# Cross attention and quantised feed-forward: seven block products in the last two token groups only, six groups as plain units

## The reference

```python
x = x + xattn(layernorm(x), ctx, Wq, Wkv)          # x: 2 x 2048 x 512, ctx: 2 x 128 x 512
h = act_qdq(layernorm(x))                          # 16-bit grid, one scale for the whole tensor
up   = act_qdq(h @ lpbq_dequant(w_up).T)           # weights 1536 x 512, 4 bits in blocks of 32
gate = act_qdq(h @ lpbq_dequant(w_gate).T)
gate = act_qdq(gate * fixed_qdq_u16(sigmoid(gate)))
o    = act_qdq(gate * up)
out  = x + o @ lpbq_dequant(w_down).T
```

## Time and profile before

| | us |
|---|---|
| median of 3 runs | 909.1 (908.61 to 911.49) |
| profiled execution | 906.48 |
| its span | 904.7 |
| TensorE, ScalarE, VectorE, GpSimd busy | 858.6, 593.1, 722.3, 202.6 |
| plain units | 130.3 to 258.6 |
| quads | 258.6 to 377.4 |
| up stage | 382.0 to 636.8 |
| first down pass and product | 645.0 to 731.5 |
| rest of the down projection | to the end |

### The profile page before, as it was taken

How to read it: one execution, slowest core, us unless ns; L and a number is a source line. 1 busy time by engine, 2 the same in 40 slices (tenths; PEclk the granted TensorE clock), 3 DMA queues, 4 the chain that set the end, 5 groups by cost and what they waited for, 6 DMA issues and landing times.

```text
span 904.7 us, 11995 instructions
## 1 busy us (share of the span) xinstructions
PE 858.6 (95%) x4072; PEld 423.6 (47%) x4072; DVE 722.3 (80%) x1009; ACT 593.1 (66%) x740; POOL 202.6 (22%) x170
## 2 busy tenths in 40 slices
PE   7999879999987999799999989999799989999998
PEld 5877554444433444344444434444344434444443
DVE  4879885689774868688996859857899997999892
ACT  2478776785673456689996859853689975455330
POOL 0099949499400088000000000000000000000000
PEclk9999979999999999999999999999999999999999
DMA  9822319753899558999439993799897897989872
GB/s 345 328 94 95 139 48 318 219 173 121 237 293 300 211 192 210 277 375 347 163 138 323 361 354 141 261 399 389 288 400 278 276 321 278 391 304 385 301 288 102
DMA packets 126469, 236.61 MB, mean 262 GB/s; under 512 B 48336, under 2 KB 66768, under 8 KB 124368
## 3 DMA queue, kind: packets, MB, share of 16 engines
q1 hardware_dynamic: 125264, 231.77, 73.5%
q10 hardware_dynamic: 1152, 4.19, 1.2%
HBM read 130.55 MB, written 95.42 MB: 250 GB/s over the span
## 4 chain that ended last, share of the span: by engine, by line
PE 59%; issue 14%; POOL 8%; DMA 6%; DVE 6%; ACT 3%; SPq 3%; POOLq 0%; ACTq 0%; DVEq 0%
PE ps L1091 27%; PE ps L1141 14%; PE ps L1042 8%; PE ps L1026 6%; PE ps L1168 3%; POOL big L858 2%; DMA big<-in_L_ffn_w_gate_dram 2%; DMA big<-big 2%; ACT big L1186 1%; POOL big L815 1%; POOL big L809 1%; DVE big L1756 1%; PE ps L1158 1%; POOL small L855 1%; DVE big L1730 1%
## 5 line engine op out<-in xcount | busy, mean ns | idle before, releaser
L1091 PE MATMUL ps<-big 128*128 (+1 forms) x1152 | 252.4, 383 | 7.1 <-DMA big<-big 4.6
L1091 PEld LDWEIGHTS ps<-big 128*128 128x128 f16 x1152 | 113.4, 99 | 146.0 <-issue 7.5
L1186 ACT ACTIVATE big<-ps 128x1024 f32<-128x1024 f32 (+2 forms) x142 | 113.9, 813 | 94.9 <-PE ps L896 25.5
L1026 PE MATMUL ps<-big 128*128 (+1 forms) x576 | 124.8, 379 | 4.1 <-ACT big L1186 3.7
L1141 PE MATMUL ps<-big 128*128 128x512 f16 x576 | 126.5, 382 | 2.3 <-DVE big L1961 2.3
L1042 PE MATMUL ps<-big 128*128 128x512 f16 x504 | 111.1, 383 | 7.7 <-DVE big L1801 5.7
L800 POOL PARTITION_ALL_REDUCE small<-small x8 | 3.3, 414 | 456.2 <-DVE small L1902 187.5
L1141 PEld LDWEIGHTS ps<-big 128*128 128x128 f16 x576 | 56.7, 99 | 71.7 <-issue 4.9
L1026 PEld LDWEIGHTS ps<-big 128*128 128x128 f16 x576 | 56.0, 98 | 72.7 <-ACT big L1186 4.6
L1122 PE MATMUL ps<-big 128*128 128x512 f16 x384 | 85.0, 384 | 5.1 <-ACT big L1471 5.1
L1042 PEld LDWEIGHTS ps<-big 128*128 128x128 f16 x504 | 49.4, 99 | 69.2 <-DVE big L1801 7.3
(11 more groups left out here) (117 smaller groups left out, 1310.5 us busy)
## 6 DMA issues: line engine op xcount, KB each, us to landing
big<-up_park SPq DMA_DIRECT2D x90, 512.0 KB, 6.5
big<-gate_park SPq DMA_DIRECT2D x48, 512.0 KB, 6.3
up_park<-big SPq DMA_DIRECT2D x48, 512.0 KB, 4.6
gate_park<-big SPq DMA_DIRECT2D x24, 512.0 KB, 2.9
gate_park<-big SPq DMA_DIRECT2D x48, 256.0 KB, 2.4
big<-in_x_dram SPq DMA_DIRECT2D x8, 1024.0 KB, 18.3
x_park<-big SPq DMA_DIRECT2D x8, 1024.0 KB, 3.9
product_park<-big SPq DMA_DIRECT2D x16, 512.0 KB, 5.6
```

The lines of the kernel that those rows point to most:

```text
L1026: mm = nc.tensor.matmul(unit_banks(n)[:, j], WG[:, x, a, k % 2, o:o + P], XT[:, g, b, k], start=(k == 0 and a + b == 0), stop=(k == KC - 1 ...
L1091: mm = nc.tensor.matmul(ps[:, b + j], WU[:, a, k, o:o + P], XT[:, g, c, k], start=(k == 0 and a + c == 0), stop=(k == KC - 1 and c == 1))
L1186: return nc.scalar.activation(dst, src, ACT.Copy)
```

## The change

Six groups are plain units and only groups 6 and 7 are quads: 36 units and 6 quads. The token sums of that one pair are made at units 24 to 26. Down pieces go to units 14, 17, 20, 23. Up weights are loaded behind units 27 to 30, their block maxima are taken at units 29 and 30, their scales at 31 and 33, and they are split at quads 1 to 4 and transposed at quads 2 to 5. A piece is now three blocks of 128 weight rows with all 512 columns (`up_rows`, `WU` and the loads are laid out for it); each piece has its own semaphore, and TensorE waits for piece 0, 1, 2, 3 at up units 0, 1, 3, 4, while ScalarE, VectorE and SyncE wait for all four (`up_turned`). At the quads' end gates 1 to 5 are fetched one by one, each behind the stores of its quad, with the last stores between them.

```diff
-FLAT_G = 4
+FLAT_G = 6
 FLAT = FLAT_G * UPG
-PAIRS = (NG - FLAT_G) // 2
-QUADS = PAIRS * UPG
+QUADS = UPG
 G_COLS = FLAT + 4 * QUADS
 SUM_AT = (8, 10, 13, 16)
 SPLIT_AT = (3, 5, 7, 9, 11, 16, 18)
-DOWN_AT = (14, 16, 19, 21)
-PARK_AT = (17, 19, 22, 24)
-TURN_AT = (19, 12)
-UP_AT = (7, 8, 9, 10)
+DOWN_AT = (14, 17, 20, 23)
+PARK_AT = (16, 19, 22, 25)
+TURN_AT = 25
+UP_AT = (1, 2, 3, 4)
+LOAD_AT = 27
+BLOCKS_AT = (29, 30)
+SCALE_AT = (31, 33)
+
+UP_PIECES = OC // 3
+UP_NEEDS = (0, 1, 3, 4)
...
-        WU = part(U0, 6144).bitcast(F16).rearrange("p (l k o) -> p l k o", l=2, k=KC)
+        WU = part(U0, 6144).bitcast(F16).rearrange("p (l h k c o) -> p l h k c o", l=2, h=UP_PIECES, k=KC, c=3)
...
+        def up_rows(l, c):
+            return natural_at(1, c // 3)[:, l].rearrange("p (k c d) -> p c k d", k=KC, c=3)[:, c % 3]
+
...
-        wu_turned, wd_turned = sem("wu_turned"), sem("wd_turned")
+        wu_0, wd_turned = sem("wu_turned"), sem("wd_turned")
+        wu_turned, WU_TURNED = [wu_0, wg_ld[1], wn_ld[2], wd_turned], (0, 16, 16, 16 * 2 * KC)
...
+        def up_turned(eng):
+            for h in range(UP_PIECES):
+                eng.wait_ge(wu_turned[h], WU_TURNED[h] + 32)
+
...
             def load_up_weights(k):
-                sp.dma_start(WN.rearrange("p (k c d) -> p k c d", k=KC, c=OC)[:, k],
-                             wu_in[:, k * P:(k + 1) * P].rearrange("(c p) d -> p c d", p=P)).then_inc(up_ld[k], 16)
+                sp.dma_start(WN.rearrange("p (c d) -> p c d", c=OC)[:, 3 * k:3 * k + 3],
+                             wu_in.rearrange("(c p) d -> p c d", p=P)[:, 3 * k:3 * k + 3]).then_inc(up_ld[k], 16)
...
+                if LOAD_AT <= u < LOAD_AT + KC:
+                    load_up_weights(u - LOAD_AT)
...
-                if q == 0:
-                    park_down_weights(KC - 1)
-                if q < 2:
-                    load_up_weights(2 * q)
-                    load_up_weights(2 * q + 1)
-                if q >= QUADS - 4:
-                    if q == QUADS - 4:
-                        sp.wait_ge(q_mm, Q_MM + done_p7(UPG * (PAIRS - 1) - 1))
-                        sp.wait_ge(t_lo, T_LO + 4 * PAIRS)
-                    turn_up_weights(q - QUADS + 4)
+                if q - 1 in UP_AT:
+                    if q - 1 == UP_AT[0]:
+                        sp.wait_ge(t_lo, T_LO + 4)
+                    turn_up_weights(UP_AT.index(q - 1))
...
             sp.wait_ge(q_mm, Q_MM + 7 * QUADS)
-            for x in (1, 3):
-                sp.wait_ge(c_st[x], C_ST + 16 * UPG)
-            for i in range(1, 6):
+            def fetch_late_gate(i):
+                for x in (1, 3):
+                    sp.wait_ge(c_st[x], C_ST + 16 * i + 16)
                 fetch_gate(i)
+
+            fetch_late_gate(1)
+            fetch_late_gate(2)
             for x in (2, 3):
                 park_half(QUADS - 1, x)
+            fetch_late_gate(3)
+            fetch_late_gate(4)
+            for x in (2, 3):
+                park_half_sign(QUADS - 1, x)
+            fetch_late_gate(5)
             for s in range(3):
                 sp.wait_ge(g_st[s], 16 * FLAT // 3)
             fetch_gate(6)
             fetch_gate(7)
-            for x in (2, 3):
...
-                            sp.wait_ge(wu_turned, 16 * 2 * KC)
+                            up_turned(sp)
...
-            pe.wait_ge(wu_turned, 16 * 2 * KC)
...
+                if n in UP_NEEDS:
+                    h = UP_NEEDS.index(n)
+                    pe.wait_ge(wu_turned[h], WU_TURNED[h] + 32)
...
+                if m == 1:
+                    copy(up_rows(0, c), WN[:, c * D:(c + 1) * D].rearrange("p (k d) -> p k d", k=KC)).then_inc(wt_hi, 1)
                 else:
-                    act.wait_ge(t_lo, T_LO + 4)
-                copy(natural(m, 0, c), WN[:, c * D:(c + 1) * D]).then_inc(wt_hi, 1)
+                    copy(natural(m, 0, c), WN[:, c * D:(c + 1) * D]).then_inc(wt_hi, 1)
...
-            act.wait_ge(wu_turned, 16 * 2 * KC)
+            up_turned(act)
...
+                if u in BLOCKS_AT:
+                    up_block_max(2 * BLOCKS_AT.index(u))
+                    up_block_max(2 * BLOCKS_AT.index(u) + 1)
+                if u == SCALE_AT[0]:
+                    block_scales(1)
+                if u == SCALE_AT[1]:
+                    common_scale(1, 3)
...
-                if 2 <= q < 4:
-                    up_block_max(2 * q - 4)
-                    up_block_max(2 * q - 3)
-                if q == 3:
-                    block_scales(1)
-                if q == 5:
-                    common_scale(1, 3)
```

More of the change, by code:

```diff
@@ L1046, in first_of @@
             def first_of(q, base):
[L1047 to L1048 removed]
+                g = FLAT_G
+                six(base + 1, q, WG[:, 1], XT[:, g, :, 2:4], True)
             def quad(q):
[L1051 to L1052 removed]
+                base, g, n = 4 * ((q + 1) % 2), FLAT_G, q
                 need(pe, c_ev, C_EV + 4 * (q - 1) if q > 1 else 0)
@@ L1344, in _ @@
                 nc.scalar.activation(sign_out[:, u % 2], gate_out[u % 3], ACT.Sign).then_inc(sign_ev, 1)
-                for pr in range(PAIRS):
-                    for j in range(4):
-                        if u == TURN_AT[pr] + j // 2:
-                            turn_hi(pr, j)
+                for j in range(4):
+                    if u == TURN_AT + j // 2:
+                        turn_hi(j)
                 if u % 2 and u < 2 * NG - 3:
```

90 lines of the change are left out of this document (39 added, 51 removed).

## The result

| | before | changed |
|---|---|---|
| median of the runs | 908.86 us (907.23 to 911.49) | 899.07 us (897.58 to 900.64), 4 runs |
| ratio | | 0.9885, 95% interval [0.9866, 0.9903] |
| profiled execution, its span | 906.48, 904.7 us | 900.64, 898.8 us |

Forecast were 904.6 us; measured were 899.1, close to rival A's 898.3. Faster, as forecast, but by 9.8 us where 4.5 stood, though inside the stated range of 897.5 to 909.0. The two profiled executions in the table lie nearer to each other (5.9 us) than the medians do (9.8 us), so places in time are compared with the second pair beside the first.

What follows compares the result with a forecast made beforehand. TensorE was taken to bound the gate stage, a ScalarE, VectorE and DMA chain the up stage to 541 us. Terms 7.8 - 3.2 - 2.7 - 6.4 = -4.5 us gave 904.6 us, range 897.5 to 909.0.

Steps and rivals of the forecast that it cites:

- rival A: Up stage: ScalarE's chain follows TensorE, so the early start is kept whole, 6.3 us; 898.3 us; chance 12%.
- Part 7: Up stage: row pieces start TensorE 6.3 us ahead, all given back before unit 30; 0 us, bounds 0 and -8.2.
- Part 1: Gate stage: 36 more matmuls at 0.2158 us each, all on the path; +7.8 us.
- Parts 2 and 3: Both plain-stage breaks shrink or go, -3.2 us (bounds 0, -3.7); the breaks entering the quads go, -2.7 us.
- Part 4: Quad 2: its 4.9 us break and 1.5 us of slow clock go as loads move; -6.4 us.
- Part 5: Plain stage: up-weight loads behind units 27 to 30 cause no break, with 8 us of cover; 0 us.
- Part 6: Quads: GpSimd's up blocks run from 309.5 to 350.6 us, 10.7 us before they are wanted; 0 us.
- the first sign of the prediction: TensorE's profile after: no break of a microsecond or more between 130 and 372 us.
- The sum to the quads' end: Parts 1 to 4 together, 7.8 - 3.2 - 2.7 - 6.4: the quads end 4.5 us earlier.
- The break before unit 30: Up stage: TensorE, ahead of ScalarE, waits 2.4 + 6.3 = 8.7 us there, the clock falling to 0.5.
- Rivals B and C: B: breaks move instead of going, 911.0 us, 14%. C: GpSimd's late blocks stop TensorE in quad 4, 914.9 us, 6%.

Runs made afterwards that it cites:

- the second pair: Both kernels run once more, unchanged, with profiles: before 908.76 us, ratio 1.0001; changed 897.43 us, ratio 0.9864.
- the spread loads: Kernel before with the four up-weight loads behind quads 0 to 3, block maxima and scales moved: 907.9 us, ratio 0.9976.
- the repeat: Changed kernel run once more, unchanged, for a second profile: 897.43 us, ratio 0.9864.
- the repeat of before: Kernel before run once more, unchanged, for a second profile: 908.76 us, ratio 1.0001.
- the version with early gates: Changed kernel with gates 39 and 40 fetched at up step 24 instead of 25: 893.83 us, then 895.74; waiting for all pieces too, 900.08.
- two loads at a time: Changed kernel with the four up-weight loads issued two behind unit 27 and two behind unit 28: 896.48 us in one run.

## Why the prediction was wrong

It was wrong in one term of the sum, Part 7; the others held within about two microseconds.

- **Part 1**, +7.8 us: right; the regular runs have the same 0.2158 us a matmul.
- **Parts 2 and 3**, -3.2 and -2.7: all three breaks went (3.7 and 2.7 us). The reason was half right: in the plain stage fewer token sums, not the new places, did it; for the entry no run tells.
- **Part 4**, -6.4: right. The break of quad 2 and its slow clock are gone, and the spread loads show that four loads in two quads made at least 4.4 of the 6.4 us.
- **Part 5**, 0: right, and with more room than the 8 us; a load took 4.6 us to land, 7.8 before.
- **Part 6**, 0: GpSimd's times to a microsecond. But I costed the pairing only from GpSimd's side. VectorE's low parts of the up weights stretch beside it: two of 128x512 take 3.77 us while GpSimd works and 1.28 after. Changed kernel, VectorE in order of time:

```profile
345.54 3.77 DVE L1658 TENSOR_TENSOR big<-big 128x512 f16<-128x512 f32 x2
...
355.74 1.28 DVE L1658 TENSOR_TENSOR big<-big 128x512 f16<-128x512 f32 x2
```

  The combine behind it is late, and that is the new break of 1.25 us in quad 3 (1.51 in the repeat). All seven profiles of the changed kernel and its variants in which the pair took 3.8 us have such a break, of 1.06 to 1.52 us; the one in which it took 2.86 has none, nor have the five of the kernel before in which it took 2.72. So the first sign of the prediction, no break of a microsecond between 130 and 372 us, did not hold. The Trainium skill (SBUF - State Buffer, "Who interferes with whom") has the rule, that a VectorE operation with two SBUF inputs and a GpSimd operation that reads SBUF shut each other out; these rows agree, and here VectorE paid.
- **The sum to the quads' end**, -4.5: -4.0 and -5.6 measured. Counted from each execution's first plain unit, and without the 1.7 us of slow clock in the repeat of before, it is -4.6 and -3.7: right.
- **Part 7**, "Given back: 6.3 of 6.3": this failed. Its bound of -8.2 was known, and I took 0 because "from 382 to 541 us ScalarE waited for TensorE for 1.9 us only". The rows said 1.9 for TensorE and 4.9 for VectorE; 4.5 of the 4.9 (eight waits of 0.56 us, up to unit 17) were TensorE's as well. The stretch is not one chain: up to unit 17 ScalarE follows TensorE, from unit 18 on late gates hold ScalarE. A head start of 6.3 us lets ScalarE go at its own 9.70 us a pair, win 5.7 to 7.0 us by unit 17 and keep a good part of it, since the fetches are ordered by up units and came earlier too. Removed alone, it costs 5.7 us by the medians and 2.5 to 4.3 by the traces. I had argued that the 12.7 us of fetch waits would not be touched by an earlier start; they became little longer (14.0 and 14.1 us), but their place moved forward with the units.
- **The break before unit 30**: forecast 8.7 us, measured 6.23 and 4.75. By my own test (not longer than 2.4 us for rival A) the result lies between the two, as the head start wins its time before unit 17 and a part of it stands as a longer break.
- **Rivals B and C** did not come: no break in the plain stage or behind the quads' entry, and no wait for GpSimd. **Rival A**, at 12%, named the right place. That its 898.3 lies so near to the 899.1 is in part luck: it has the whole 6.3 us kept, and the traces show less, with 2 to 4 us of the medians' difference not located in them. Its reason "against", the 1.9 us, was the misread row.

What stays open: ScalarE's first copy in the up stage stood at 385.5 to 386.7 us in seven executions of the changed kernel and its variants, and at 383.7 in the changed kernel with TensorE waiting for all pieces, though its quads ended only 1 us earlier. In the changed kernel its first gate step waits for the last transposes; in that run it waited for the gate's scale (2.3 us, VectorE L1708), the transposes having landed sooner. No run here says why. An earlier start of ScalarE can't be what made that run slower, so the 5.7 us do not come from it.

## What to carry to other kernels

A wait that the trace puts to one engine may belong to another that ends at the same moment: divide the period between like instructions by each engine's work for it (here 10.36 us = 48 matmuls), take the engine that it fits as the likely pace-maker, and test it by shortening the work of each. Split a long stage where its pace-maker changes before pricing a head start; one won ahead of a stretch that follows the sped-up engine was kept there, and later waits that are ordered by progress moved along with it, though not all of it survived them.

## What the runs showed of the hardware

- The length of an idle time alone did not tell whether the clock fell. Behind 2.43 us before unit 30 it did, and behind 2.19, 2.26, 2.27, 2.43 and 2.44 us before the plain stage, in five executions. Windows at its start in the run where TensorE waited for all pieces in the version with early gates (2.26 us before the stage) and in the changed kernel (0.26 us):

```profile
131.00:133.00 2.00, 2.00 (x6) 0.72 (x5) 1.97 (x5) 2.00 (x2) 0.00 (x0) 0.50 0.00 0
```

```profile
131.00:133.00 2.00, 2.00 (x10) 0.77 (x10) 1.93 (x6) 2.00 (x3) 0.00 (x0) 1.00 0.00 0
```

  There it costs 188.33 - 186.64 = 1.69 us each time. But breaks of 2.00 us in the plain units cost nothing (15.71 - 0.16 - 72 x 0.2158 = 0.0), and neither did one of 2.62 us at the same place in the kernel before with spread loads:

```profile
237.37 15.71 PE L1025 MATMUL ps<-big 128*128 x72 [2.62 <-ACT big L1185]
```

  What TensorE had done before differs: 20 units without a break before the 2.62 us, short f32 matmuls with idle times between them before the 2.19 to 2.44 us. At the plain stage the clock's level just before differs too. With two loads at a time (2.19 us before the stage), and then in the changed kernel:

```profile
126.00:128.00 2.00, 1.79 (x17) 1.60 (x15) 1.14 (x5) 0.60 (x1) 0.38 (x1) 1.00 0.00 0
```

```profile
126.00:128.00 2.00, 1.86 (x9) 1.89 (x10) 1.43 (x4) 0.74 (x2) 0.00 (x0) 0.50 0.00 0
```

  Where the clock was full there, the short matmuls were done early, TensorE waited over 2 us, and the stage began slow; where it was at 0.50, they took longer, the wait was under 1 us, and no such price was paid. Which of the two an execution has makes one part of the spread between executions of one kernel.
- The price of a fall before unit 30 did not follow the length of the break: the run of 432 matmuls less 0.16 and 432 x 0.2158 gives 1.7 us behind 2.43 and 3.39, 1.3 behind 3.88, 1.7 and 2.2 behind 4.75 in two executions, 2.9 behind 4.81, 2.6 behind 6.23 and 2.3 behind 6.47. (For the 2.43 the prediction has 1.6; its own sum gives 1.7.)
- Two VectorE operations of 128x512 with both inputs in SBUF took 1.28 us alone and 2.72, 2.86 or 3.77 us beside GpSimd's up blocks, by how the blocks fell against them.
